# Causal attention maxima on one core: the mask leaves TensorE's products and goes to VectorE as an add on the diagonal pieces

## The reference, cut to what matters

```python
q = q + pe[None, None]
k = k + pe[None, None]
causal = jnp.tril(jnp.ones((T, T), dtype=bool))
scores = jnp.einsum('bhtd,bhsd->bhts', q, k) / jnp.sqrt(jnp.asarray(D, q.dtype))
scores = jnp.where(causal[None, None], scores, jnp.asarray(-jnp.inf, q.dtype))
probs = jax.nn.softmax(scores, axis=-1)
attn = jnp.einsum('bhts,bhsd->bhtd', probs, v)
```

## Time and profile before

| | |
|---|---|
| median of 3 runs | 733.39 us (732.24 to 735.25) |
| the profiled execution: its time, its span | 734.77 us, 733.0 us |
| PE busy | 654.5 us (89%) |
| DVE busy | 504.9 us (69%) |
| POOL busy | 503.1 us (69%) |
| ACT busy | 449.2 us (61%) |
| line 407, the units' maxima on DVE | 320 times, 181.0 us |
| line 485, the mask products on PE | 128 times |

### The profile page before, as it was taken

One profiled execution on the slowest core, in us unless ns is written; L12 is line 12 of the kernel. 1 busy time (PEld: TensorE's weight loads), 2 busy tenths in 40 slices (PEclk: granted clock), 3 DMA queues, 4 the chain that ended last, 5 costly groups with the idle time before them and its releaser, 6 DMA issues. The chain is left out here.

```text
span 733.0 us, 10119 instructions
## 1 busy us (share of the span) xinstructions
PE 654.5 (89%) x3215; PEld 497.5 (68%) x3215; DVE 504.9 (69%) x1048; ACT 449.2 (61%) x626; POOL 503.1 (69%) x289
## 2 busy tenths in 40 slices
PE   5789999999999999999999999999877899989873
PEld 4557777777777777777677777777667687666651
DVE  3577667667766766866776676674187978877684
ACT  3436666676666666667667666667636577756551
POOL 6016887887878788788787778879943456667560
PEclk9979999999999999999999999999988899999995
DMA  7423211222112221122211232103300000000000
GB/s 186 110 64 70 61 44 45 46 69 60 44 43 49 69 58 44 44 51 69 55 44 44 53 71 51 45 1 91 98 2 1 0 1 1 0 16 0 14 1 29
DMA packets 27460, 33.75 MB, mean 46 GB/s; under 512 B 6897, under 2 KB 13842, under 8 KB 27282
## 3 DMA queue, kind: packets, MB, share of 16 engines
q1 hardware_dynamic: 27410, 33.14, 19.0%
HBM read 6.84 MB, written 1.05 MB: 11 GB/s over the span
## 5 line engine op out<-in xcount | busy, mean ns | idle before, releaser
L313 POOL TENSOR_TENSOR probs_l<-probs,probs_h 128x1024 fp32r<-128x1024 f32 (+1 forms) x160 | 347.5, 2177 | 132.0 <-PE o_ps L536 73.6
L407 DVE TENSOR_REDUCE m_part<-max_ps 128x1 f32<-128x512 f32 (+2 forms) x320 | 181.0, 605 | 111.0 <-PE max_ps L483 79.6
L350 ACT ACTIVATE probs<-scores 128x1024 f32<-128x1024 f32 (+1 forms) x160 | 150.3, 940 | 153.9 <-PE scores L511 96.7
L536 PE MATMUL o_ps<-probs_h,v 128*128 128x512 f32 (+5 forms) x640 | 185.2, 373 | 24.6 <-DVE oh L386 24.1
L353 ACT ACTIVATE probs_h<-scores 128x1024 fp32r<-128x1024 f32 (+1 forms) x160 | 149.8, 936 | 0.0
L536 PEld LDWEIGHTS o_ps<-probs_h,v 128*128 128x128 f32 (+1 forms) x640 | 95.9, 162 | 48.3 <-issue 20.0
L814 POOL TENSOR_TENSOR hid_lo<-hid,hid_hi 128x512 fp32r<-128x512 f32 x64 | 86.6, 1359 | 55.0 <-ACT hid_hi L894 42.3
L510 PE MATMUL scores<-q,k 128*128 128x512 f32 (+1 forms) x320 | 122.8, 384 | 0.0
L511 PE MATMUL scores<-q,k 128*128 128x512 f32 (+1 forms) x320 | 116.9, 365 | 0.0
L536 PE MATMUL o_ps<-probs_l,v 128*128 128x512 f32 (+1 forms) x320 | 116.4, 364 | 0.0
L483 PE MATMUL max_ps<-k,q 128*128 128x512 f32 (+2 forms) x320 | 103.1, 398 | 7.4 <-DVE m_part L407 6.2
(11 more groups left out here) (195 smaller groups left out, 986.9 us busy)
## 6 DMA issues: line engine op xcount, KB each, us to landing
k<-qk SPq DMA_DIRECT2D x96, 128.0 KB, 2.3
q<-qk SPq DMA_DIRECT2D x96, 128.0 KB, 2.3
q<-m_turn SPq DMA_DIRECT2D x128, 0.5 KB
v_all<-L_ffn_ew SPq DMA_DIRECT2D x2, 768.0 KB, 6.5
pos<-positions SPq DMA_DIRECT2D x1, 1024.0 KB, 6.8
out<-v_all SPq DMA_DIRECT2D x4, 256.0 KB, 2.3
acc<-L_attn_Wqkv SPq DMA_DIRECT2D x2, 256.0 KB, 3.9
v_all<-L_attn_Wo SPq DMA_DIRECT2D x2, 256.0 KB, 6.4
```

The lines of the kernel that those rows point to most:

```text
L313: pool.tensor_tensor(probs_l[:, p % 2, :, lo:CH], probs[:, p % 2, :, lo:CH], probs_h[:, n % 3, :, lo:CH], ALU.subtract).then_inc(S["probs_ ...
L350: act.activation(probs[:, p % 2, :, lo:CH], scores[:, p % 2, :, lo:CH], ACT.Exp, scale=D ** -0.5).then_inc(S["probs_ready"], 1)
L407: dve.tensor_reduce(m_part[:, r, j:j + 1], max_ps[:, u % 2, 0:width], AX.X, ALU.max).then_inc(S["tile_max_ready"], 1)
L536: last = pe.matmul(o_ps[0:rows, lo:CH], v, pr, start=(p == PAIR0[c] and j == 0 and k == 0), stop=(p == PAIR0[c + 1] - 1 and j == 1 and k = ...
```

## The change

The mask product is left out, so that every unit is one product. A new mask `mask_qk` (128x128, float32, in SBUF) is made once by GpSimd. For a diagonal unit DVE adds it to the last 128 columns of the product and writes the sum into `m_diag[:, r, :]`; what lies ahead of these 128 columns (nothing for r = 0) is reduced by an instruction of its own into column 1 of `m_part`. At a chunk's end one reduction takes the maxima of the four pieces of `m_diag` into column 0, and the old one over `m_part` waits for it.

```diff
-        m_part = sb("m_part", [P, TPC, NC])
+        m_part = sb("m_part", [P, TPC, NC + 1])
+        m_diag = sb("m_diag", [P, TPC, P])
+        mask_qk = sb("mask_qk", [P, P])
...
-            pool.wait_ge(S["masks_made"], 2)
+            pool.memset(mask_qk[:], 0.0).then_inc(S["masks_made"], 1)
+            pool.wait_ge(S["masks_made"], 3)
+            pool.affine_select(out=mask_qk[:], in_=mask_qk[:], compare_op=ALU.is_ge, fill=NEG, base=0,
+                               pattern=[[-1, P]], channel_multiplier=1).then_inc(S["masks_made"], 1)
...
-            dve.wait_ge(S["maxima_cleared"], 1)
+            dve.memset(m_part[:], NEG).then_inc(S["maxima_cleared"], 1)
+            dve.wait_ge(S["maxima_cleared"], 2)
+            dve.wait_ge(S["masks_made"], 6)
...
                         dve.wait_ge(S["max_scores_ready"], of * NU + u + 1)
-                        dve.tensor_reduce(m_part[:, r, j:j + 1], max_ps[:, u % 2, 0:width], AX.X, ALU.max).then_inc(S["tile_max_ready"], 1)
+                        if j < c:
+                            dve.tensor_reduce(m_part[:, r, 2 + j:3 + j], max_ps[:, u % 2, :], AX.X, ALU.max).then_inc(S["tile_max_ready"], 1)
+                        elif r == 0:
+                            dve.tensor_tensor(m_diag[:, r, :], max_ps[:, u % 2, 0:P], mask_qk[:], ALU.add).then_inc(S["tile_max_ready"], 1)
+                        else:
+                            dve.tensor_tensor(m_diag[:, r, :], max_ps[:, u % 2, width - P:width], mask_qk[:], ALU.add)
+                            dve.tensor_reduce(m_part[:, r, 1:2], max_ps[:, u % 2, 0:width - P], AX.X, ALU.max).then_inc(S["tile_max_ready"], 1)
                         if u + 1 == UNIT0[c + 1]:
                             n = of * NC + c
                             dve.wait_ge(S["tile_max_ready"], of * NU + u + 1)
+                            dve.tensor_reduce(m_part[:, :, 0], m_diag[:], AX.X, ALU.max).then_inc(S["diagonal_max_ready"], 1)
+                            dve.wait_ge(S["diagonal_max_ready"], n + 1)
                             wait(dve, S["row_max_turned"], n)
-                            dve.tensor_reduce(m_max[:, 0:TPC], m_part[:, :, 0:c + 1], AX.X, ALU.max, negate=True).then_inc(S["row_max_ready"], 1)
+                            dve.tensor_reduce(m_max[:, 0:TPC], m_part[:, :, 0:c + 2], AX.X, ALU.max, negate=True).then_inc(S["row_max_ready"], 1)
...
-                last = pe.matmul(max_ps[:, u % 2, 0:n], q1[:, tile:tile + P], k1[:, h % 2, ks], start=True, stop=(j < c))
-                if j == c:
-                    last = pe.matmul(max_ps[:, u % 2, width - P:width], mask_kq[:, P:2 * P], ident_b[:], start=False, stop=True)
+                last = pe.matmul(max_ps[:, u % 2, 0:n], q1[:, tile:tile + P], k1[:, h % 2, ks], start=True, stop=True)
```

More of the change, by code:

```diff
@@ L202, in attention @@
             v_copied v_high_ready v_low_ready qk_projected qk_positioned qk_high_ready qk_low_ready
-            max_operands_moved score_operands_moved max_scores_ready tile_max_ready row_max_ready row_max_turned
+            max_operands_moved score_operands_moved max_scores_ready tile_max_ready diagonal_max_ready row_max_ready row_max_turned
             max_row_moved scores_ready probs_ready probs_high_ready probs_low_ready pv_done
@@ L292, in _ @@
                                pattern=[[1, 2 * P]], channel_multiplier=-1).then_inc(S["masks_made"], 1)
-            pool.wait_ge(S["masks_made"], 4)
+            pool.wait_ge(S["masks_made"], 6)
             pool.memset(q2[D:P, :].bitcast(F32), 0.0).then_inc(S["rows_beside_qk_made"], 1)
@@ L565, in section @@
                         pv_pair(h - 1, NP - 2 + p)
-            pe.wait_ge(S["masks_made"], 4)
+            pe.wait_ge(S["masks_made"], 6)
             section(-1)
```

## The result

The changed kernel takes 737.15 us (median of 14 runs, 731.63 to 738.77) where the kernel before takes 733.69 (14 runs, 730.63 to 735.77). The ratio is 1.0048, with a 95% interval of 1.0029 to 1.0068: slower by about 0.5%, where 731.6 us and no change were forecast. The profiled execution took 736.21 us, span 734.5.

What follows compares the result with a forecast made beforehand. PE was taken as the bound except at four waits a section for `oh`, where DVE (sometimes ACT) holds it. 8.9 - 5.5 - 0.6 - 1.0 = 1.8 us less gave 731.6 us, with an 8-in-10 range of 727.5 to 738.5.

Steps and rivals of the forecast that it cites:

- the rivals for slot 2: Slot 2: the delay stays hidden, 724.5 to 728.8 us (chance 0.08), or PE's clock falls, 737 to 740 (0.22).
- The sum: Whole kernel: 8.9 gained, less 5.5 (slot 0), 0.6 (section 0) and 1.0 (before head 0), makes 1.8 us less.
- the rival: Slot 2: longer waiting halves PE's clock for 3.4 us, 1.7 us a fall; three to five falls, 737 to 740; chance 0.22.
- the stretch after: Around slot 2: with 1.0 us more waiting, PE busy falls from 2.97 to about 2.0 of 4.00 us.
- the masks inside slot 2's chain: Units 23 and 27: skipping their masks gains nothing and only lengthens PE's slot 2 wait, by 0.25 us.
- Masks: Ten of a section's 16 masks count, 0.125 us each: 1.25 us in sections 0 to 6, 8.9 gained in all.
- DVE's prices: On DVE: `m_diag` reduction 0.69 us (0.72 with its wait), 128-column add 0.28, each split 0.07.
- Slot 0: Head of slot 2's chain: split and reduction delay PE by 0.79 us in sections 1 to 7, 5.5 us lost.
- The absorbed places: Chunk ends in slots 8, 10 and 14: DVE's spare time takes the delay, costing nothing; slot 14 is closest.
- PE's other waits: Slots 4, 8 and 14: PE's waits for `oh` grow by 0.12 to 0.25 us.
- Section 0: Section 0: PE's 0.43 us wait for unit 24 grows by 0.79 less 0.21 us, a loss of 0.6.
- Before head 0: From 40.53 us, behind chunk 1's end: 0.79 us and two or three splits, a loss of 1.0 us.

Runs made afterwards that it cites:

- e1_fill: Changed kernel plus five unread 512-column PE products ahead of the wait for `oh` in slot 2 of sections 1 to 7; 730.86 us, ratio 0.9956.
- e5_nomask_add: Kernel before without mask products, plus an unread 4 x 128 DVE reduction at all four chunk ends, no splits or small adds; 735.68 us, ratio 1.0038.
- e2_nomask: Kernel before with its mask products removed and nothing in their place; 722.63 us, ratio 0.985.
- e3_add_slot0: Kernel before, masks kept, plus an unread 4 x 128 DVE reduction at chunk 2's end (slot 0); 740.82 us, ratio 1.0094.
- e4_add_slot10: Kernel before, masks kept, plus an unread 4 x 128 DVE reduction at chunk 0's end (slot 10); 732.84 us, ratio 0.9991.
- e6_more: Changed kernel plus a further 4 x 64 DVE reduction at chunk 2's end (slot 0); 737.26 us, ratio 1.0059.
- e10_start: Kernel before without the 11 mask products of the 22 units ahead of section 0, all others kept; 733.27 us, ratio 0.9997.

## Why the prediction was wrong

**The step that failed** is the choice among the rivals for slot 2. The sum has no term for PE's clock: the prediction took it that the clock, which "stayed full behind 2.97 of 4.00 around slot 2", would stay full with 1.0 us more of waiting, and gave the fall 0.22. In its place the runs show falls of 1.5 us each, three in the profile and about four a run, 6.3 us in all (737.15 less e1_fill's 730.86). The rival's text has the place, the side, "three to five" falls and 737 to 740 us (737.15 measured). Its size was set at 1.7 us a fall, half of 3.4; measured are 1.5. That the falls are the loss is shown by e1_fill, the change without them; e5_nomask_add has them without the splits and the small add.

Two readings went wrong in it. The first is the stretch after, put at "about 2.0 of 4.00" with about 2.1 us of idle time at the wait. Measured are 2.57 of 4.00 and 1.18 us: between starts the stand is 2.16 us, but a part of it lies in stops ahead of the first and of the second maximum product, 0.16 and 0.10 us. So the rival was right on the fall with too long a stand, which is in part luck. Its comparison of two rows could not have decided the matter either: 2.57 of 4.00 lies nearer to the row where the clock stayed (2.97 of 4.00) than to the one where it fell (1.62 of 3.40).

The second is that the masks inside slot 2's chain were put down as costing only a longer wait of PE. e2_nomask has neither these masks nor the delay, e3_add_slot0 has the masks and the delay, e5_nomask_add has the delay without the masks. Only the last has falls, three in its profile, and a mean clock as low as the changed kernel's. A delay in the other chunk ends, which e5_nomask_add also has, is no likely cause, since slot 10's alone brought none (e4_add_slot10); those in slots 8 and 14 were not tried alone. So the removed TensorE work is a part of the cause as far as these runs can tell, together with the delay.

The Trainium skill has both shapes, in "TensorE: Matmul & The Clock Gate": "HAM oscillation — how this bites in real kernels" is one long wait in each round, "A second HAM failure mode: psum-queue depth-cycling" short idle times between groups of products that put the clock down and up again. The trace is nearer to the second, with waits of 0.16 and 1.18 us; but it is not every round here, three sections of seven.

**What held.** *Masks:* the gain of a section is that of ten of 16, 0.13 each (e2_nomask); 0.125 was forecast. *DVE's prices:* 689 ns for 0.69, 282 for 0.28; the split 0.07 by the chain's 0.79. The estimate of 0.59 us worked out from the errata table of "VectorE: DVE Perf Modes" in the Trainium skill is not what this reduction takes, 0.69. The prediction said that the trace disagrees with the same page's section "The DRAIN you can't avoid"; that section of the Trainium skill adds that an operation that is not held starts earlier, and the 0.08 us of overlap agree with that. *Slot 0:* 0.79 us a section, of which 0.72 are the reduction: in e3_add_slot0, which has no split, the chain on DVE is longer by 0.73 (6.39 against 5.66) and the section by 0.80; the 0.07 between lies in several slots, 0.01 to 0.03 each. *The absorbed places:* slot 10 is shown by e4_add_slot10 (0.06 a section). For slots 8 and 14, which no run tried alone, section 3 speaks: behind e2_nomask the changed kernel is 0.80 us at slot 2's value product, 0.82, 0.86 and 0.85 at those of slots 4, 8 and 14, and 0.89 at the section's end. *PE's other waits:* longer by 0.06 in slot 4, by nothing in slot 8 and by 0.19 in slot 14 of section 3; 0.12 to 0.25 were forecast.

**What was off beside it.** *Section 0* is shorter by 0.9 us (60.65 to 59.75), where 0.65 was forecast (1.25 less 0.6). This is no proof of the term: the clock was at 0.50 up to 53.1 us before and up to 51.3 after, so section 0 has other half-clock time in the two profiles. (The prediction has the clock fall before head 0 only; it reaches into section 0, which starts at 48.29.) *Before head 0* I put a loss of 1.0 us. The first score product comes at 48.31, before at 48.29. In that part rows of single profiles differ by over 1 us, so the term is within what one trace can't tell. With it at nothing the sum is -2.8, and the change without falls measured -3.1 (730.86 against 733.97 in that comparison).

**What stays open.** First, why the clock falls in sections 2, 4 and 5 and not in 1, 3 and 6 of the changed kernel. In sections 2 to 6 the stand has the same instructions and the same idle times; in section 1 PE was busy even less, 2.34 of 4.00 us, and the clock stayed. What differs is the moment. In each kept trace all changes of the clock, those outside attention too, lie on one even beat. The start of the value product behind the stand, counted from the nearest beat (minus is ahead of it), is:

| | sections with a fall | sections 1 to 6 without |
|---|---|---|
| changed kernel | -0.45, -0.11, 0.07 us | 0.49, 0.61, 0.88 us |
| e5_nomask_add | -0.54, -0.16, -0.02 | -1.29, 0.49, 1.06 |
| e6_more | -0.17, 0.27, 0.39 | 0.79, 0.91, 1.25 |

The moment alone is not enough: e2_nomask has stands at -0.17 and -0.40 and the kernel before has one at -0.17, and no fall. In e3_add_slot0's profile no stand of sections 1 to 6 comes nearer than 0.95 us to a beat, so this profile by itself does not show that its stand is safe; the mean clock of its six runs is what speaks for that. I found this order in the traces afterwards. No experiment here shifts only that moment, so it is not shown to be the cause.

Second, the 2.0 us that e2_nomask gained beyond its sections (11.3 less 9.3): e10_start, without the masks in the part where they seemed to lie, shows nothing of it.

## What to carry to other kernels

Price an instruction by what is queued behind it: the same 0.69 us reduction cost 0.80 us a section at the head of a chain that ends in a TensorE wait, and 0.06 in another place. TensorE work that lies inside such a chain was no gain when it was removed (e2_nomask), and with a longer chain beside it a loss, since the engine's idle time grew and the clock fell for 3.4 us behind it; so a change that lengthens a stand of TensorE needs a look at the granted clock in short stretches, not in the page's 40 slices. When work moves to a helper engine, move it first off the chain (1.5% here, where the change as made lost 0.5%), and as a test put products that nobody reads into the engine's idle time. One profile without a fall is weak evidence that the clock is safe; compare the mean clock of several runs.

## What the runs showed of the hardware that I had not expected

- Five products of 512 columns that nobody reads made the kernel 0.9% faster (737.15 to 730.86 us), because PE's clock then stays at 1.00 through slot 2.
- The clock fell behind idle times of 0.16 and 1.18 us, with PE busy 2.57 of the 4.00 us ahead; before the change it was 2.97 of 4.00 and one wait of 1.03 us, and the clock fell in none of sections 1 to 7.
- Behind stands of the same instructions and idle times the clock fell in some sections and not in others: in the changed kernel where the stand ended between 0.45 us ahead of and 0.07 behind the beat on which all changes of the clock in the trace lie, and not where it ended 0.49 us or more behind it.
- A longer stand (0.63 us ahead of the maximum products where it was 0.16) did not bring more falls: 3.2 us of them against 6.3, both profiles with three.
